# The relation stage: GpSimd adds the two heads that ScalarE scales, and each turned block is two transposes instead of three

## The reference, cut to what matters

```python
q = (x[sub] @ Wq.T + bq).reshape(-1, 8, 64)
k = (x[obj] @ Wk.T + bk).reshape(-1, 8, 64)
att = ((q * k).sum(-1) / sqrt(64)).T
scores = zeros((8, n, n)).at[:, sub, obj].set(att)
scores = where(mask, -inf, scores)     # only edges of the graph stay
scores = scores.at[:, di, di].set(1e-07)
attn = softmax(scores, axis=2)
aggregator_factor = attn.sum(axis=0) / 8
return aggregator_factor @ x           # and x is added to it
```

## Time and profile before

| | us |
|---|---|
| median of 3 runs | 3774.04 |
| lowest, highest | 3762.97, 3775.52 |
| the profiled execution | 3772.07 |
| its span, first to last instruction | 3770.3 |
| the relation stage in it | from about 3150 to the end |

### The profile page before, as it was taken

One profiled execution on the slowest core, in us unless ns is written; L12 is line 12 of the kernel. 1 busy time (PEld: TensorE's weight loads), 2 busy tenths in 40 slices (PEclk: granted clock), 3 DMA queues, 4 the chain that ended last, 5 costly groups with the idle time before them and its releaser, 6 DMA issues. The chain is left out here.

```text
span 3770.3 us, 56703 instructions
## 1 busy us (share of the span) xinstructions
PE 3378.9 (90%) x20628; PEld 2047.1 (54%) x20628; DVE 3201.0 (85%) x5502; ACT 2818.1 (75%) x3508; POOL 1389.7 (37%) x1048
## 2 busy tenths in 40 slices
PE   7799999986968976899999975989999898999999
PEld 3699999743434433444444432468888443444444
DVE  3699999679999999599999998389998414999996
ACT  5699999559999999389999982368776334666664
POOL 0387444104555556136565552145552110000000
PEclk9999999998989988999999987999999999999999
DMA  6721111120111113221101022410100211111110
GB/s 234 269 84 31 31 36 25 52 70 27 54 32 42 42 44 102 78 81 46 39 20 28 26 73 70 154 26 21 21 22 10 86 72 61 48 51 56 48 51 17
DMA packets 166328, 224.45 MB, mean 60 GB/s; under 512 B 90418, under 2 KB 102672, under 8 KB 162928
## 3 DMA queue, kind: packets, MB, share of 16 engines
q1 hardware_dynamic: 147152, 178.22, 15.1%
q0 software_dynamic: 18896, 42.46, 3.5%
HBM read 148.36 MB, written 72.00 MB: 58 GB/s over the span
## 5 line engine op out<-in xcount | busy, mean ns | idle before, releaser
L1819 DVE SCALAR_TENSOR_TENSOR adjT<-adjT,mid 128x2048 bf16<-128x2048 f32 x440 | 1034.8, 2352 | 13.9
L604 ACT ACTIVATE steepz<-s1b,thr_h 128x512 bf16<-128x512 f32 (+1 forms) x928 | 774.3, 915 | 32.5 <-DVE A L675 20.3
L1715 ACT ACTIVATE adjT<-adjT,nmid 128x2048 bf16<-128x2048 f32 x250 | 498.4, 1994 | 3.4 <-POOL nmid L1757 3.4
L1719 ACT ACTIVATE adjT<-adjT 128x2048 bf16<-128x2048 bf16 x250 | 477.9, 1912 | 6.0
L758 PE MATMUL acc<-V,B 128*128 128x198 bf16 x4096 | 442.5, 251 | 34.2 <-DVE B L677 14.1
L765 PE MATMUL acc<-V,adjT 128*128 128x99 bf16 (+1 forms) x5248 | 415.5, 217 | 0.0
L1773 POOL TENSOR_SCALAR reach<-above,lack 128x1 f32<-128x1 f32 x202 | 234.2, 1159 | 472.9 <-ACT lack L1722 472.7
L1775 POOL TENSOR_SCALAR nmid<-reach,steps,nmid 128x1 f32<-128x1 f32 x202 | 369.4, 1829 | 21.2
L765 PEld LDWEIGHTS acc<-V,adjT 128*128 128x128 bf16 x5248 | 340.5, 98 | 40.2 <-issue 0.7
L758 PEld LDWEIGHTS acc<-V,B 128*128 128x128 bf16 x4096 | 341.2, 98 | 37.6 <-issue 23.3
L1574 PE MATMUL psX<-parts,block 128*128 128x512 bf16 x1536 | 347.9, 382 | 10.5 <-POOL ident L209 4.1
(11 more groups left out here) (322 smaller groups left out, 6214.2 us busy)
## 6 DMA issues: line engine op xcount, KB each, us to landing
rows<-in_adj_dram SPq DMA_DIRECT2D x16, 1024.0 KB, 8.3
s1b<-sT_dram SPq DMA_DIRECT2D x32, 512.0 KB, 3.7
block<-adj_dram SPq DMA_DIRECT2D x32, 512.0 KB, 4.4
plain_table<-rows POOLq DMA_DIRECT2D x16, 512.0 KB, 8.1
adj_dram<-adjT POOLq DMA_DIRECT2D x4, 2048.0 KB, 21.6
veil_table<-fill POOLq DMA_DIRECT2D x64, 128.0 KB
y_dram<-yo SPq DMA_DIRECT2D x32, 256.0 KB, 2.0
adjT<-adj_dram SPq DMA_DIRECT2D x4, 2048.0 KB, 16.4
```

What stands on the lines that cost most here:

```text
L604: act.activation(steepz[:, m % RELUS, :], s1b[:, q % 4, :], ACT.Relu, bias=thr_h[:, u, 1, j:j + 1], scale=STEEP).then_inc(relu_ready, 1)
L1715: act.activation(junk_s[:, u, :], expd[:, slot[i], :], ACT.Relu, bias=col(nmid, i), accum_out=col(above, i)).then_inc(sums_ready, 1)
L1719: act.activation(junk_s[:, u, :], junk_s[:, u, :], ACT.Sign, accum_out=col(over, i)).then_inc(sums_ready, 1)
L1819: link(dve.scalar_tensor_tensor(junk[:, :], e, col(mid, i), e, ALU.is_gt, ALU.mult, accum_out=found))
```

## The change

GpSimd gets the sum of heads 6 and 7: for tile n it waits until ScalarE has scaled both, and adds head 7 into head 6 in four instructions of 512 columns. The output DMAs stay in GpSimd's queue; the one of tile n-3 now follows the adds of tile n. TensorE waits for the sum (`summed`) instead of `scaled`, and each turned block is two transposes, of `G(t, 5)` and `G(t, 6)`.

```diff
@@ relation_stage
+            summed = self.sem(st, "summed")
             def parts(t):
-                return [G(t, h) for h in range(SUM, H)]
+                return [G(t, SUM), G(t, SUM + 1)]
...
                 pool.memset(std[:, :], REL_STD).then_inc(std_ready, 1)
-                for t in range(NT):
-                    pool.wait_ge(xo_ready, t + 1)
-                    pool.dma_start(out[tile(t), :], xt[:, t % 2, :]).then_inc(x_out[t % 2], 16)
+                for n in range(NT + 3):
+                    if n < NT:
+                        pool.wait_ge(scaled, SCALED * (n + 1))
+                        a, b = G(n, SUM + 1), G(n, SUM + 2)
+                        for c in range(4):
+                            cols = slice(c * 512, (c + 1) * 512)
+                            pool.tensor_tensor(a[:, cols], a[:, cols], b[:, cols], ALU.add).then_inc(summed, 1)
+                    if n >= 3:
+                        t = n - 3
+                        pool.wait_ge(xo_ready, t + 1)
+                        pool.dma_start(out[tile(t), :], xt[:, t % 2, :]).then_inc(x_out[t % 2], 16)
...
                     if gp == 0:
                         pe.wait_ge(weighed, SUMMED * (t + 1))
-                        pe.wait_ge(scaled, SCALED * (t + 1))
+                        pe.wait_ge(summed, 4 * (t + 1))
...
-                                           start=(n == 0), stop=(n == SCALED), is_transpose=True)
+                                           start=(n == 0), stop=(n == 1), is_transpose=True)
```

## The result

| | before | changed |
|---|---|---|
| median, us | 3774.8 | 3938.9 |
| lowest to highest | 3763.0 to 3776.3 | 3936.5 to 3943.6 |
| the profiled execution | 3772.1 | 3943.6 |
| period of a tile in the steady state | 36.49 | 50.2 |

The ratio is 1.0443, 95% interval 1.043 to 1.0456: 164 us slower, where 3941 us was forecast.

What follows compares the result with a forecast made beforehand. VectorE was taken to bound the kernel, TensorE close behind. Late query loads 150, early tiles and finish 5 + 10, and the end 4 made 169 us on the profiled 3772.07, giving 3941 us; range 3888 to 3990.

Steps and rivals of the forecast that it cites:

- The bound: Last stage, steady period: VectorE busy 35.67 of 36.49 us sets the period, TensorE (36.18) at its heels.
- the 0.43 allowed: Steady state: fewer transposes can save only VectorE's 0.43 us of waits per period, at most 7 us over 16 tiles.
- The chain: Tile to tile, through adds, late output, x load and query load: 50.1 us instead of 36.49, 13.6 more.
- a whole turn of 1.28: GpSimd's four adds: VectorE takes one 1.28 us instruction between them, so 5.14 + 1.28 = 6.42 us.
- The count: Query tiles of tiles 5 to 15 come late: 11 x 13.6 = 150 us.
- tiles 1 to 4: No load late there, but adds meet VectorE's two-input instructions: 1.28 us x 4 = 5 us.
- The finish of tile 13: Behind tile 15, its x load waits behind tile 11's output: 48.1 us after VectorE's start instead of 37.8, 10 us.
- The end: Last tile: adds alternate with VectorE's chain, TensorE's last 32 products start at +28.3, not +23.6; transposes save 1; net 4 us.
- Rival A: Same chain, but TensorE restarts at full clock, 2.11 us: period 48.4, total 3921 us; chance 0.21.
- Rival B: SyncE's late load stays hidden; only add collisions cost VectorE, two adds of 1.28 per tile: 3814 us; chance 0.08.
- Rival C: Faster: TensorE's 2 us per tile decides, loads come within the old period, adds never hold VectorE: 3763 us; chance 0.04.
- Rival D: Adds at their slow 1.711 us, loads landing late, clock low longer: chain 54.7 us, total 4002 us; chance 0.05.

Runs made afterwards that it cites:

- e3: Kernel before with two transposes per turned block, no adds, head 7 left out of the result: 3766.9 us, ratio 0.9984.
- e2: Kernel before with GpSimd's new queue order (outputs behind the wait for both scalings), no adds, three transposes: 3867.0 us, ratio 1.0250.
- e5: Changed kernel with TensorE kept busy by 12 unread products ahead of the query wait, tiles 5 to 15: 3933.7 us.
- e6: Changed kernel with SyncE's mask load of the next tile issued ahead of the wait for the output: 3937.7 us.
- e7: Changed kernel with both TensorE kept busy in the gap and the mask load ahead of the output wait: 3917.8 us.
- e1: Changed kernel with the output DMA of tile n-2 ahead of the adds of tile n in GpSimd's queue: 3792.1 us, ratio 1.0052.
- e9: Changed kernel with e1's output order, ScalarE's second scaling right behind its first, each add held until a chosen weigh ended: 3773.1 us, ratio 0.9997.
- e10: As e9, but the last tile has no adds and three transposes per block: 3765.9 us, ratio 0.9982 to the kernel before.

## Why the prediction was right, point by point

**The bound.** VectorE sets the period: e3 took 2.0 us per tile from TensorE and the period fell by 0.20, within the 0.43 allowed.

**The chain.** The terms as forecast, and as the turn from 3543.61 to 3593.94 shows them:

| | forecast | measured |
|---|---|---|
| VectorE's start to the end of the second scaling | 34.37 | 34.37 |
| four adds, up to the issue of the output | 6.42 | 5.95 |
| output, issue to the issue of the x load | 2.3 | 2.32 |
| x load ahead of the query load | 0.43 | 0.36 |
| query load, issue to TensorE's start | 2.8 | 3.42 |
| TensorE's start to VectorE's | 3.78 | 3.91 |
| sum | 50.1 | 50.3 |

Two terms are off and cancel, so that 50.1 came so close is in part luck. I gave the adds a whole turn of 1.28; a turn is what is left of the running instruction and came to 0.9. And I took the query load's 2.8 us from a period in which it is alone; in the changed kernel, with three more loads issued beside it, its median landing is 3.2 (the same in e2, e5, e6 and e7, which have the same bunch; that the bunch is the cause was not tried). Both were within the bounds stated.

A third thing was left out and cost nothing, by luck: the chain has no term for the mask load, which VectorE needs as well as the scores. The prediction was to be wrong if anything but TensorE's scores ended VectorE's idle time, and in five of eleven the profile names the mask. e6, with the mask out of the way, is 1 us faster, so at the low clock the scores were no earlier than the mask. Had the clock been full, the mask would have set the last term, as it does in e5.

**The count.** Eleven late query loads, as said: 11 x 13.7 = 151 us.

**The rest.** In tiles 1 to 4 the adds cost 2.6 us over the three periods between 3214.41 and 3326.52 (5 forecast for four). The finish of tile 13 came 46.4 us after VectorE's start of tile 15 (48.1 forecast), 8.7 over before. The end, from there to the last finish, took 45.6 us against 40.1, so 5.5 where 4 was forecast. Timelines of the end of the changed kernel, VectorE, GpSimd and TensorE:

```profile
3897.37 9.65 DVE L2468 SCALAR_TENSOR_TENSOR Gb<-Gb,r 128x1024 f32<-128x1024 f32 x8
3907.05 1.24 DVE L2474 SCALAR_TENSOR_TENSOR Gb<-ident,own,Gb 128x128 f32<-128x128 f32 x1
3916.82 0.75 DVE L2413 SCALAR_TENSOR_TENSOR xt<-psO,fin,xt 128x512 f32<-128x512 f32 x1 [8.52 <-DMA xt<-xc]
```

```profile
3903.28 8.58 POOL L2269 TENSOR_TENSOR Gb<-Gb 128x512 f32<-128x512 f32 x4 [17.35 <-ACT Gb L2371]
```

```profile
3917.62 6.39 PE L2328 MATMUL psO<-B,attnT 128*128 128x512 f32 x8 [1.90 <-DVE xt L2413]
```

Adds and weighs did not alternate as I had it: the weighs took their 9.65 and the adds 8.58, one of them 4.87, so here GpSimd was the one to wait. The adds ended at +21.4 all the same (21.5 forecast), and TensorE's last 32 products began at +27.1 (28.3 forecast). The miss lies behind them. I had 1 us saved there; it took 1.9 us more than before (18.5 from there to the last finish, against 16.6). TensorE had been idle 2.71 us ahead of the last tile's transposes and 1.90 ahead of the products, the granted clock was 0.50 from 3915 to 3920, and the first eight products took 6.39 us where they took 3.60. The low clock that I had put into every late tile I left out of the end.

Together 151 + 3 + 9 + 5 = 168; the stage also began 3.5 us later in this execution (its first query load at 3154.1, not 3150.6), which makes the 171.5 between the two profiled executions (169 forecast; the medians differ by 164).

**Rival A** (full clock at the restart) fell with the rows on the clock: 3.91 us, not 2.11. e5 and e7 add what neither it nor the forecast had: full clock alone gives 5 us and not 20, as the mask load stands behind. A's 3921 needs both, and e7 with both measures 3918. **Rival B** (only the collision left) is nearly e1, which it would have put at 3814; it has 3792, since its two turns cost 0.75 and 0.9 us and not 1.28 each, and 0.4 of that falls where VectorE waited before. **Rival C** (faster) has the size of e3. **Rival D** did not happen: in each late turn one add took 2.2 us, but the four of a late turn together took 5.9, not 8.1, and the query loads landed after 3.1 to 4.1 us, median 3.2.

## What to carry to other kernels

An engine's queue is in order for its DMA issues too: work put ahead of a DMA delays whoever waits for its landing, and whatever stands behind that one in its own queue. Before an idle engine is given work, follow each DMA that it issues to the wait on its landing and to the load behind that wait, and count how early that load is; here it had a whole period to spare, and lost it with 13.7 us more. Where a moved piece must run beside VectorE, start it beside instructions that were not held here, the reductions with one SBUF input. And when two profiles are compared at their end, measure from a point inside the stage: their stages begin some microseconds apart.

## What the runs showed of the hardware that was not expected

- Who waits when adds and two-input instructions of VectorE meet back to back is not fixed: in e9's last tile eight weighs took 13.69 us beside four adds in 8.40, in the changed kernel's last tile eight weighs took 9.65 and one add took 4.87. What decides it was not tried.
- A small instruction is held about as long as a large one: in e1 `diagonal`, 128x128, took 1.23 us instead of 0.35, 0.9 more, and a weigh of 128x1024 took 2.03 instead of 1.28, 0.75 more.
- After 12.2 us without work TensorE's first eight score instructions took 3.78 us, 0.47 each. After the 5.75 us before the stage ten took 4.48, 0.45 each, with the granted clock at 0.50 until 3158 and at 1.00 from there: the longer idle time cost hardly more.
- At the end, shorter idle times were enough. With 2.53 (e9) and 2.71 us (changed kernel) ahead of the last tile's transposes the granted clock fell to 0.50, and eight products took 5.46 and 6.39 us instead of 3.60; with 1.74 us it stayed at 1.00, and in e9 too, but after the same 1.74 us it fell to 0.50 in e10: the length of the idle time alone does not decide it.
